# Cross-attention steps by head half instead of by sequence, in a fused decoder layer on one core

## The reference

```python
x = x + attn(layernorm(x))                  # causal, one head of 256, rotary
x = x + xattn(layernorm(x), ctx, ctx)       # 8 heads of 128, windows of 64 keys, dilations 1,1,2,2,4,4,8,8
x = x + moe(layernorm(x))                   # moe(t) = t + gated sum of the best 2 of 8 experts 256 -> 512 -> 256

# xattn, per head h: q, k, v = query@Wq[h].T+bq, key@Wk[h].T+bk, value@Wv[h].T+bv
# scores = q . k over the head's window (others masked), softmax, out = attn . v
# result: concat(heads) @ Wc.T + bc
```

## Time and profile before

| What | us |
|---|---|
| Median of 3 runs | 492.69 (492.01 to 493.49) |
| The profiled execution, whole | 493.77 |
| its span, first to last instruction | 491.9 |
| TensorE busy | 457.1 (93% of the span) |
| VectorE busy | 352.0 (72%) |
| ScalarE busy | 280.2 (57%) |
| GpSimd busy | 175.9 (36%) |
| DMA | 54.37 MB, 111 GB/s mean |

### The profile page before, as it was taken

How to read it: one execution, slowest core, us unless ns; L and a number is a source line. 1 busy time by engine, 2 the same in 40 slices (tenths; PEclk the granted TensorE clock), 3 DMA queues, 4 the chain that set the end, 5 groups by cost and what they waited for, 6 DMA issues and landing times.

```text
span 491.9 us, 11187 instructions
## 1 busy us (share of the span) xinstructions
PE 457.1 (93%) x3670; PEld 323.7 (66%) x3670; DVE 352.0 (72%) x837; ACT 280.2 (57%) x715; POOL 175.9 (36%) x184
## 2 busy tenths in 40 slices
PE   5999989999999999999999999989799999999960
PEld 2456469856458966556895646778676787888840
DVE  5754667796866778686678688898668885555476
ACT  4273756626547535555761665563666777877830
POOL 1230124040204313012504020234346877777541
PEclk9799999999999999999999999999999999999995
DMA  8901000034230031621003424608113247223655
GB/s 324 376 13 45 0 2 0 29 103 160 98 129 0 0 128 43 213 85 44 1 0 128 122 92 131 246 16 350 47 45 122 79 135 268 78 81 84 195 197 213
DMA packets 20410, 54.37 MB, mean 111 GB/s; under 512 B 3365, under 2 KB 9774, under 8 KB 19600
## 3 DMA queue, kind: packets, MB, share of 16 engines
q1 hardware_dynamic: 16336, 43.32, 24.7%
q0 software_dynamic: 3744, 9.47, 6.7%
q10 hardware_dynamic: 288, 1.05, 0.6%
HBM read 36.98 MB, written 17.76 MB: 111 GB/s over the span
## 4 chain that ended last, share of the span: by engine, by line
PE 45%; issue 25%; DVE 14%; POOL 8%; DMA 5%; DVEq 1%; POOLq 0%; ACT 0%; ACTq 0%; SPq 0%
PE pj L1469 16%; PE op L1702 7%; PE pj L1683 4%; DMA picked<-wch,dst_row 3%; PE sc L1658 2%; POOL pn L461 2%; POOL picked L490 2%; DMA cst<-rows,src_row 2%; PE pj L1795 2%; POOL rstd L430 1%; PE sc L1556 1%; DVE stats L769 1%; POOL cst L479 1%; PE ov L1469 1%; PE tpA L1805 1%
## 5 line engine op out<-in xcount | busy, mean ns | idle before, releaser
L1469 PE MATMUL pj<-up,up_f 128*128 128x512 f16 x480 | 109.6, 383 | 2.8 <-DVE down L1313 1.1
L1469 PEld LDWEIGHTS pj<-up,up_f 128*128 128x128 f16 x480 | 46.3, 99 | 59.5 <-DVE rope L939 4.6
L679 ACT ACTIVATE p<-sc,nm 128x128 f32<-128x128 f32 x128 | 45.4, 369 | 38.3 <-DVE nm L1308 38.1
L461 POOL TENSOR_TENSOR pn<-p,inv 128x256 f32<-128x256 f32 x64 | 37.9, 614 | 79.3 <-DVE inv L1261 79.3
L479 POOL DMA_INDIRECT cst<-rows,src_row x39 | 48.7, 1248 | 19.9 <-issue 7.6
L490 POOL DMA_INDIRECT picked<-wch,dst_row x39 | 41.5, 1064 | 26.4 <-DVE wch L1252 9.9
L430 POOL TENSOR_TENSOR rstd<-veps,nhalf 128x4 f32<-128x4 f32 (+1 forms) x13 | 12.7, 975 | 103.2 <-DVE veps L777 102.9
L551 ACT ACTIVATE down<-pj,bias 128x512 f32<-128x512 f32 x48 | 32.6, 686 | 26.5 <-PE pj L1469 26.3
L1469 PE MATMUL pj<-up_f,up 128*128 128x512 f16 x192 | 43.4, 379 | 0.0
L1702 PE MATMUL op<-wch,outs 128*128 128x256 f16 x240 | 40.2, 273 | 0.0
L1683 PE MATMUL pj<-pT,v 128*128 128x128 f32 x256 | 34.3, 279 | 1.3 <-DVE outs L1279 0.8
(11 more groups left out here) (265 smaller groups left out, 1025.5 us busy)
## 6 DMA issues: line engine op xcount, KB each, us to landing
raws<-in_staged SPq DMA_DIRECT2D x12, 512.0 KB, 5.4
split<-halved SPq DMA_DIRECT2D x12, 512.0 KB, 3.2
down<-split SPq DMA_DIRECT2D x4, 1024.0 KB, 8.6
rows<-row SPq DMA_DIRECT2D x4, 528.0 KB
small<-in_x SPq DMA_DIRECT2D x4, 512.0 KB, 3.6
up<-in_ctx SPq DMA_DIRECT2D x4, 512.0 KB, 4.8
v<-in_w SPq DMA_DIRECT2D x2, 1024.0 KB, 9.2
resid<-outs SPq DMA_DIRECT2D x4, 512.0 KB
```

Of the source, the lines that this page charges most:

```text
L461: pool.tensor_tensor(pn2[:, n % 2, k], p2[:, n % 2, k], inv2[:, n % 2, k].unsqueeze(2).to_broadcast([P, 2, P]), ALU.mult)\
L679: last = act.activation(p2[:, s, i, :], sc[s][:, i * P:(i + 1) * P], ACT.Exp, bias=nm2[:, s, i:i + 1], scale=1.0, accum_out=sum2[:, s, i:i ...
L1469: last = pe.matmul(out, w(c), v(c), start=(i == 0), stop=(i == len(terms) - 1))
```

## The change

Step n is now sequence n % 4 and head half n // 4: all four sequences with heads 0 to 3, then all four with heads 4 to 7. Four queries instead of five stand ahead of `scores(0)`; the other four (heads 4 to 7, needed from step 4 on) come one behind each of the first four score groups, and ScalarE takes all of them out. The weights of the first four steps are transposed by TensorE, those of the last four by VectorE (before: even and odd). The output products of a step (12, `add_heads`) stand between the steps as soon as its half of the heads is there; two sequences share a bank, their sums stay open over the first half of the steps (op for sequences 0 and 1; ov, in the last group tpB, for 2 and 3). VectorE's and ScalarE's lists are written anew, with other distances; the early conversions move between the steps. The diff, cut to its core:

```diff
+        LATE_Q = ((0, 13), (1, 13), (0, 14), (0, 15))
+        WEIGHTED = ((1, 14), (1, 15), (0, 16), (1, 16), (0, 17), (1, 17), (0, 18), (1, 18))
...
 # GpSimd, back
+                    if 2 <= n < 6:
+                        pool.wait_ge(tpA_full, TPA * g + 3 + n - 1)
+                    if n >= 6:
+                        pool.wait_ge(blocks_turned, 4 * g + n - 5)
...
 # ScalarE, back
+                project(g, 2, range(2, 4))
+                for n in range(8 + 3):
+                    if n >= 3:
+                        m = n - 3
+                        k, use = WEIGHTED[m]
                         if m >= 4:
+                            act.wait_ge(heads_added, 4 * g + m - 3)
+                        act.wait_ge(pj_full[k], PJ * g + use)
+                        copy(oTh[:, m % 4].rearrange("p a b -> p (a b)"), pj[k][:], MID).then_inc(o_hi, 1)
+                    if n < 8:
+                        s = n % 2
+                        if n >= 2:
+                            act.wait_ge(norm2, 16 * g + 2 * n - 2)
+                        act.wait_ge(neg2, 8 * g + n + 1)
+                        for i in range(4):
+                            last = act.activation(p2[:, s, i, :], sc[s][:, i * P:(i + 1) * P], ACT.Exp,
...
+                        last.then_inc(sc_free[s], 1)
+                    if n < 4:
+                        k, use = LATE_Q[n]
...
+                        act.wait_ge(pj_full[k], PJ * g + use)
+                        act.activation(qT[:, 4 + n, :], pj[k][:], ACT.Identity, bias=bias[:, 4 + n:5 + n],
+                                       scale=DOWN).then_inc(pj_free[k], 1)
+                    if more and n == 3:
+                        early(g + 1, 1)
+                    if more and n == 5:
                         early(g + 1, 0)
+                    if not more and n == 8:
                         up_high()
                         act.preload_act_table(ACT.Silu)
+                if more:
+                    part_high(g, 0)
+                    turned(g + 1)
+                else:
+                    act.wait_ge(small_in, 48)
+                    copy(b2, b2f, UP).then_inc(b2_hi, 1)
...
 # VectorE, back
+                for n in range(8):
+                    s = n % 2
+                    if n >= 3:
+                        outputs_low(n - 3)
+                    dve.wait_ge(sc_full[s], (SC[0] * g + 1, SC[1] * g)[s] + n // 2 + 1)
+                    dve.tensor_reduce(nm2[:, s, :], sc[s][:].rearrange("p (b t) -> p b t", b=4), AX, ALU.max,
+                                      negate=True).then_inc(neg2, 1)
+                    if n >= 1:
+                        transposed(n - 1)
+                    sums(n)
+                    if more and n == 4:
                         early(g + 1, 3)
+                    if more and n == 6:
                         early(g + 1, 2)
 # as before, for not more: old_counts at n == 1, old_tiles at 2, old_places at 3, old_lanes at 4, lane_rows at 5, 6, 7
...
+                outputs_low(5)
+                transposed(7)
+                if more:
+                    outputs_low(6)
+                    residual(0, op)
+                    residual(1, op)
+                    outputs_low(7)
+                    turned(g + 1)
+                    residual(2, ov)
+                    residual(3, ov)
+                    part_low(g, 0)
+                else:
                     sources(TABLE_OLD, FULL, 0)
+                    outputs_low(6)
+                    residual(0, op)
                     residual(1, op)
+                    outputs_low(7)
                     tile_experts(full_first, full_n, FULL, 0)
                     dve.wait_ge(op_free, OP * g + 2 + 2)
                     norm(3, G - 1, x2, HALVES[0])
+                    residual(2, tpB)
+                    residual(3, tpB)
                     pack(0, WORDS_FULL)
                     weights_low()
                     normed(3, G - 1, x2, HALVES[0])
                     rows_low_half(0)
-                    residual(3, sc1)
                     targets(FULL, 0)
...
 # TensorE, back
+                project(g, 2, range(4))
+                def late_query(j):
+                    k, use = LATE_Q[j]
+                    pe.wait_ge(pj_free[k], PJ * g + use - 1)
+                    n0 = 2048 + P * (4 + j)
+                    three(pj[k][:], lambda c: w2h[:, c, n0:n0 + P], lambda c: w2l[:, c, n0:n0 + P],
+                          lambda c: xTh[:, c, :], lambda c: xTl[:, c, :]).then_inc(pj_full[k], 1)
...
+                def add_heads(m):
+                    (k, use), half, b = WEIGHTED[m], m // 4, m % 4
+                    dst = op if b < 2 else ov if more else tpB
...
+                    pe.wait_ge(pj_free[k], PJ * g + use)
+                    for i in range(4):
+                        for j, (o, w) in enumerate(((oTh, wch), (oTl, wch), (oTh, wcl))):
+                            last = pe.matmul(dst[:, b % 2 * D:b % 2 * D + D], o[:, m % 4, i, :], w[:, 4 * half + i, :],
+                                             start=(m in (0, 2) and i == 0 and j == 0), stop=(half == 1 and i == 3 and j == 2),
+                                             skip_group_check=True)
+                    last.then_inc(heads_added if half == 0 else op_full, 1)
+                for n in range(8):
+                    scores(n)
+                    if n < 4:
+                        late_query(n)
+                    if n == 0 and not more:
+                        ranks(slice(0, OLD), 1, USE)
+                    if 1 <= n < 5:
+                        turn_quad(n - 1)
+                    if n >= 2:
+                        weighted(n - 2)
+                    if n >= 3:
+                        add_heads(n - 3)
+                weighted(6)
+                add_heads(5)
+                if more:
+                    turn_tokens_high(g + 1)
+                else:
+                    table(JO, FULL, 1, JO // 8, RANK_OLD)
+                weighted(7)
+                add_heads(6)
+                if more:
+                    turn_tokens_low(g + 1)
+                add_heads(7)
```

More of the change, by code:

```diff
@@ L166, in decoder @@
         room = Room(outs)
-        oTh, oTl = (room.cells(2 * H * P, F16).rearrange("p (s h t) -> p s h t", s=2, h=H) for _ in range(2))
+        oTh, oTl = (room.cells(2 * H * P, F16).rearrange("p (s h t) -> p s h t", s=4, h=4) for _ in range(2))
         x1, x2 = room.take(GB, D), room.take(GB, D)
@@ L648, in back @@
                     spare_high(2)
-                project(g, 2, range(2, 5))
-                for n in range(8 + 4):
-                    if n >= 4:
-                        m = n - 4
-                        hh = 4 * (m % 2)
-                        if m >= 4:
-                            act.wait_ge(op_full, OP * g + 2 + m // 2 - 1)
-                        act.wait_ge(pj_full[m % 2], PJ * g + PROJ + m // 2 + 1)
-                        copy(oTh[:, (m // 2) % 2, hh:hh + 4, :].rearrange("p a b -> p (a b)"), pj[m % 2][:], MID)\
-                            .then_inc(o_hi, 1)
-                    if more and n == 8:
+                project(g, 2, range(2, 4))
@@ L660, in back @@
                         early(g + 1, 0)
-                    if more and n == 11:
-                        part_high(g, 0)
-                        turned(g + 1)
-                    if not more and n == 6:
+                    if not more and n == 8:
                         up_high()
-                    if not more and n == 8:
                         act.preload_act_table(ACT.Silu)
-                    if not more and n == 10:
-                        act.wait_ge(small_in, 48)
-                        copy(b2, b2f, UP).then_inc(b2_hi, 1)
@@ L682, in back @@
-                    last.then_inc(sc_free[s], 1)
-                    if more and n == 0:
-                        early(g + 1, 1)
+                if more:
[4 more added lines that the diff above has]
+                    copy(b2, b2f, UP).then_inc(b2_hi, 1)
             act.wait_ge(w1_in, 16)
@@ new lines, in weighted @@
+                def weighted(m):
+                    (k, use), half, b = WEIGHTED[m], m // 4, m % 4
+                    if m < 4:
+                        pe.wait_ge(tpA_free, TPA * g + 3 + m + 1)
+                    else:
+                        pe.wait_ge(blocks_turned, 4 * g + m - 3)
+                    pe.wait_ge(pj_free[k], PJ * g + use - 1)
+                    for i in range(4):
+                        h = 4 * half + i
+                        last = pe.matmul(pj[k][:, i * P:(i + 1) * P], v2[:, b, h * DH:(h + 1) * DH],
+                                         pT2[:, m % 2, i, :], start=True, stop=True)
+                    last.then_inc(pj_full[k], 1)
@@ new lines, in add_heads @@
+                def add_heads(m):
+                    (k, use), half, b = WEIGHTED[m], m // 4, m % 4
+                    dst = op if b < 2 else ov if more else tpB
+                    if m == 0:
+                        pe.wait_ge(wc_lo, 1)
```

(10 more changed lines are left out.)

191 lines of the change are left out of this document (51 added, 140 removed).

## The result

The changed kernel takes 510.73 us (median of 4 runs, 509.92 to 511.95) where the kernel before took 492.74 beside it: slower by a ratio of 1.0369, 95% interval 1.0342 to 1.0396. I had forecast 506.4. The direction and the place are as forecast, the size is 4.3 us short, and the time lies just outside the range of 499.0 to 510.5.

The account below looks back on a forecast made before the run. It took TensorE to bound the first three backs and VectorE the last. Early backs 9.36 + fronts 1.38 + last back 3.8 + port 0.9 = 15.4, corrected to 13.7: 507.5 profiled, 506.4 median; eight in ten 499 to 510.5.

Parts of the forecast that it names:

- three early backs and fronts, without the clock: First three groups: 9.36 us lost in the backs, plus 1.38 as each next front waits for VectorE, 0.46 a group.
- walk "0.44 too long": The same addition for the old order ended the second group's back 0.44 us too late; taken off four times, 15.4 to 13.7.
- last back, maxima to targets: Last back, from first maxima to targets: targets 3.8 us later, plus 0.9 for the port.
- TensorE's work: Same in both orders, so an early back cannot win more than the short waits TensorE still has there.
- the ring: Steps 3 to 7: VectorE and ScalarE work in turns; early-back turns of 3.94, 4.89, 4.08, 4.30 and 4.09 us.
- the start: Every back, around R, the start of the first maxima: TensorE runs dry ahead of the first quad, 1.9 us lost.
- the port's 0.9: Last back: old_places and old_lanes meet GpSimd's normalization at the shared SBUF port, +0.9 us.
- the fourth rival: First group: TensorE's clock falls behind a new wait of 3.2 us; +3 us, 509.4; chance 0.11.
- From profile to median: The earlier profiled execution was 1.1 us over the median, so 507.5 as a profile became 506.4 as a median.
- TensorE covers nothing of the ring: Rival: TensorE covers the ring, so only the start (+0.4 in two groups) and last back (+4.7) stay; 498; chance 0.15.
- A wait under 0.41 at the sums: Faster rival: the wait at the sums, put at 1.06 us a step, is hidden if under 0.41; 489.4; chance 0.05.
- GpSimd does not win the port: Rival: GpSimd wins the port, nine VectorE products each wait some 1.2 us; +10.8 more, 517; chance 0.05.

Follow-up runs that it names:

- only_last_back: First three backs as in the kernel before on all engines, only the last back as in the changed kernel; 498.37 us, ratio to before 1.0127.
- fill_wait: Changed kernel with VectorE's other work of a step (early conversions, routing work) moved ahead of that step's sums; 503.15 us, ratio to before 1.0224.
- the run with the zeros: Changed kernel with four added matmuls of zeros on TensorE ahead of the first quad of every back; 509.70 us, ratio to before 1.0352.
- the dose: Changed kernel with an added VectorE reduction of about 0.6 us behind the sums of steps 3 to 6 in the first three backs; 515.39 us.
- fill_tail: On top of fill_wait, the expert-weight conversion in the first three backs moved into waits ahead of the last low part; 501.29 us, ratio to before 1.0173.

## Why the prediction was right in direction and short in size

The prediction added 15.4 us, took off 1.8, and forecast +13.7 for the profiled execution, +17.1 was measured (spans 491.9 and 509.0). By its own terms:

| term | predicted | measured |
|---|---|---|
| three early backs and fronts, without the clock | 9.36 + 1.38 = 10.74 | 3.78 + 3.79 + 3.20 = 10.77 |
| walk "0.44 too long", four times | -1.8 | 0 |
| clock in the first group | 0 (rival: +3) | +1.64 |
| ahead of the first maxima | 0 | -0.78 |
| last back, maxima to targets | 3.8 + 0.9 = 4.7 | 6.18 |
| behind the targets | 0 | -0.71 |

The differences ahead of the first maxima and behind the targets are no larger than what executions differ by here, so they are not put down to the change: over all the kernels, with either kind of early back, the first maxima start between 64.56 and 65.60, and from the targets to the end of the span it takes 143.80 to 146.22.

- **TensorE's work, the ring and the start**: right in mechanism and in size. The agreement of 10.74 and 10.77 to 0.03 is luck all the same: the 3.20 of the third group is 0.43 too small, since the last group's first maxima come that much sooner also where the early backs are unchanged (79.78 for 80.21 in only_last_back), and this covers the amount by which the walk was short. The next front starts 36.05 behind R in the second group (35.90 predicted), 36.22 in the third, the turns are 3.92, 4.87, 4.30, 4.29 and 4.06 where I had 3.94, 4.89, 4.08, 4.30 and 4.09. The start is right in sum and wrong in its parts: TensorE does not stand 1.9 us ahead of the quad but 0.65 ahead of the first scores (ScalarE's eviction of the early queries, which I had not seen) and 0.81 ahead of the quad; in the first group 0.65 and 2.19 where I had 3.2. In steps 2 and 3 VectorE's wait is at the transposition, for TensorE's quad, and not at the sums.
- **The failed step** is the 1.8 us taken off: "0.44 too long; I take this off four times". A correction from the old order was carried over to the new one without a reason, and to the last back, for which it had not been worked out. In the new order the walk was not 0.44 too long but 0.15 and 0.32 too short in the second and third group. That is four tenths of the 4.3. The likely reason is that the old back ends on TensorE and the new one on VectorE and ScalarE; no run tests that. The rest of the 4.3 is about 1.5 from the last back, 1.0 from the step from profile to median, and 0.15 that is left of the clock, which I kept out of the sum, once the start and the end of this execution are taken off it.
- **The last back** was 1.5 short; 0.46 of that only changes its column, since I counted from a first maxima 0.46 earlier (305.92) and the measured ones came that much sooner behind the third group's. From sums(2) to sums(7) took 23.67 where 22.47 and most of the port's 0.9 were counted, and sums(2) itself came 0.8 later behind R: ahead of it the transposition waits 1.04 and 0.37 for TensorE's quads, which the walk had hidden, and `old_counts` meets the port. The port term itself was right: `old_places` and `old_lanes` take 2.18 and 2.68 here and 2.01 and 1.91 in fill_wait, 0.94 more. Not counted were `old_counts`, 1.10 for 0.65 (0.72 for 0.26 at L1091), and `old_tiles`, 1.55 for 1.00, which was slow in the rows of before already (1.48 in the earlier trace rows).
- **The clock** was the fourth rival, at 0.11. It fell, and cost 1.64 (85.96 less the 84.32 of the run with the zeros). Against it stands that it had not fallen between 10 and 18 us, where the earlier trace rows of before has 0.57 and this run 1.00, and the first maxima came 0.78 earlier. That isn't the change's doing: in the six profiles with 0.57 or 0.58 there they start at 65.40 to 65.60, in the seven others at 64.56 to 65.11, and kernels with unchanged early backs are in both. Of seven profiles with the changed early backs, four have the fall in the first group (the change itself, and those with the filling, with filling and tail, and with the dose).
- **From profile to median** I took off 1.1, the distance in the kernel before. Here the profiled execution took 510.81, as good as the median.
- **The other rivals** are out. TensorE covers nothing of the ring behind step 5 (the gaps of 0.81, 0.57 and 0.92). A wait under 0.41 at the sums would have made it faster: it is about 1. GpSimd does not win the port in the early backs, nor against the `lane_rows` of the last, where its normalization takes 2.01; it does win it against some of the small routing rows there.

Still open: how much of the 2.1 us that an early back keeps over before, with filling and tail (82.28 against 80.18), is the start alone. TensorE's gaps in the second group of fill_tail are 1.45 at the start and 0.28 and 0.97 ahead of output products, so the start is not all of it. No kernel here covers it; it would take other work for TensorE behind the first scores.

## What to carry to other kernels

When an instruction moves, look at what waits behind it on its own in-order queue, and follow the circle until it closes: here the sums, moved half a step ahead, made two engines work in turns, and each lost what the other took. Read the price of such a circle step by step, since which engine closes it changed here with each extra job. The cheap remedy is to put independent work ahead of the wait (where this also takes work away from another engine's, as in the last back, look at the rows before you call it all wait); a second remedy for the same wait can cost more than it gives.

And do not carry a correction from one order of the work to another without a reason why it should hold there.

## What was not expected of the hardware

- TensorE's clock fell behind waits of 0.65 and 2.2 us in four profiles and held at 1.00 behind the same waits in two others, with the same instructions on TensorE up to there. The Trainium skill, page "TensorE: Matmul & The Clock Gate", section "What's actually happening", has the clock follow how busy TensorE has lately been; a half clock behind one wait is in line with that. In these profiles the same wait gave both outcomes, so it could not be told from the wait alone.
- Distances between the same places repeat to 0.01 or 0.02 us from kernel to kernel (group distances of 80.17, 80.16, 80.17 and 80.18 in four kernels with the same early backs), while the medians of the same kernel before lay between 491.95 and 492.75. For questions of half a microsecond the distances in the timeline are the better instrument.
